# Loading TensorE's address registers for all tiles of a phase at once, in place of one in front of each tile

## The reference, cut to what matters

```
x = _layer_norm(src + attn, ln1_g, ln1_b)
keys = (x @ router_w + router_b)[..., 0]
expert_idx = jnp.remainder(jnp.floor(keys).astype(jnp.int32), N_EXPERTS)
for e in range(N_EXPERTS):
    h = jax.nn.relu(x @ W1[e] + b1[e])          # 128 -> 512
    y = h @ W2[e] + b2[e]                       # 512 -> 128
    ff_out = ff_out + jnp.where((expert_idx == e)[..., None], y, 0.0)
return _layer_norm(x + ff_out, ln2_g, ln2_b)
```

## Time and profile before

| | |
|---|---|
| median of 3 runs | 363.2 us (363.07 to 365.33) |
| profiled execution | 363.53 us |
| its span | 361.7 us, so 1.8 us lie around it |
| TensorE busy | 277.0 us (77%) |
| VectorE busy | 243.1 us (67%) |
| ScalarE busy | 176.1 us (49%) |
| GpSimd busy | 144.8 us (40%) |
| 16 DMA engines | 65 GB/s on average |

### The profile page before, as it was taken

How to read it: one execution, slowest core, us unless ns; L and a number is a source line. 1 busy time by engine, 2 the same in 40 slices (tenths; PEclk the granted TensorE clock), 3 DMA queues, 4 the chain that set the end, 5 groups by cost and what they waited for, 6 DMA issues and landing times.

```text
span 361.7 us, 9124 instructions
## 1 busy us (share of the span) xinstructions
PE 277.0 (77%) x3299; PEld 209.8 (58%) x3299; DVE 243.1 (67%) x677; ACT 176.1 (49%) x352; POOL 144.8 (40%) x333
## 2 busy tenths in 40 slices
PE   2665686786876826898689999998986997869970
PEld 1243454455554513576377757677865777768860
DVE  5997698888798594365257648768751465737781
ACT  2323988977998763244534624463331132314420
POOL 2126566556466360131024005703300421655665
PEclk9998889988998987699899989999997598869995
DMA  5899900000000000000000000100300352465410
GB/s 151 233 338 336 287 3 1 0 2 0 0 3 2 0 0 2 0 4 2 2 2 3 5 2 2 63 2 32 92 18 2 98 164 63 120 181 164 142 53 19
DMA packets 21875, 23.42 MB, mean 65 GB/s; under 512 B 1826, under 2 KB 18496, under 8 KB 21832
## 3 DMA queue, kind: packets, MB, share of 16 engines
q1 hardware_dynamic: 17720, 14.68, 13.8%
q10 hardware_dynamic: 2736, 4.98, 4.8%
q0 software_dynamic: 1376, 3.18, 2.5%
HBM read 10.74 MB, written 12.29 MB: 64 GB/s over the span
## 4 chain that ended last, share of the span: by engine, by line
PE 44%; DVE 27%; POOL 12%; issue 9%; ACT 3%; DMA 2%; DVEq 1%; POOLq 1%; ACTq 0%; SPq 0%
PE bank L802 9%; PE scores L775 7%; PE scores L772 6%; DVE mneg L1371 5%; POOL ln_tmp L456 5%; DVE pair_st L1251 5%; DVE early L1245 4%; PE scores L931 4%; PE bank L946 4%; PE bank L614 3%; PE bank L708 2%; DVE early L1263 1%; PE scores L640 1%; DVE early L346 1%; DVE st L278 1%
## 5 line engine op out<-in xcount | busy, mean ns | idle before, releaser
L1099 ACT ACTIVATE probs<-scores 128x1024 f32<-128x1024 f32 x32 | 32.8, 1025 | 67.0 <-PE scores L779 67.0
L1371 DVE TENSOR_REDUCE mneg<-scores 128x8 bf16<-128x1024 f32 x32 | 39.2, 1224 | 26.9 <-PE scores L772 23.6
L1245 DVE TENSOR_TENSOR_SCAN early<-a_both,bank 128x512 f32<-128x512 f32 x32 | 38.9, 1215 | 4.6 <-issue 4.3
L1379 DVE RECIPROCAL sums<-bank 128x128 f32<-128x128 f32 x16 | 15.3, 958 | 32.9 <-PE bank L802 32.8
L431 POOL TENSOR_SCALAR a_both<-early 128x508 f32<-128x508 f32 x32 | 19.5, 611 | 34.9 <-ACT early L1005 31.0
L779 PE MATMUL scores<-mnegT,pick 32*128 32x128 bf16 x256 | 30.4, 224 | 0.0
L653 PE MATMUL scores<-ident,early 128*128 128x128 f32 x64 | 16.8, 329 | 15.7 <-DVE early L1263 14.8
L1156 ACT ACTIVATE h_bwd<-bank,vec 128x128 f32<-128x128 f32 x19 | 8.7, 457 | 40.6 <-PE bank L614 36.5
L614 PE MATMUL bank<-ident,early 128*128 128x128 f32 x136 | 24.2, 308 | 3.9 <-DVE early L346 1.6
L456 POOL TENSOR_TENSOR ln_tmp<-ln_tmp,minus_half 128x8 f32<-128x8 f32 x16 | 26.4, 1648 | 1.3
L653 PEld LDWEIGHTS scores<-ident,early 128*128 128x128 f32 x64 | 10.4, 170 | 27.1 <-issue 27.1
(11 more groups left out here) (239 smaller groups left out, 766.9 us busy)
## 6 DMA issues: line engine op xcount, KB each, us to landing
sorted_rows<-blank SPq DMA_DIRECT2D x1, 8710.0 KB, 31.7
w_of<-in_L_ffn_W_dram ACTq DMA_DIRECT2D x19, 256.0 KB, 2.8
late<-sorted_rows SPq DMA_DIRECT2D x15, 130.0 KB, 2.8
x_rows<-in_x_dram SPq DMA_DIRECT2D x4, 256.0 KB, 3.1
w_s<-in_L_ffn_W_dram SPq DMA_DIRECT2D x4, 256.0 KB, 3.7
x_rows<-sorted_rows SPq DMA_DIRECT2D x4, 130.0 KB, 2.4
ctx_rows<-in_ctx_dram SPq DMA_DIRECT2D x1, 256.0 KB, 3.2
ctx_rows<-in_L_ffn_b_dram SPq DMA_DIRECT2D x1, 256.0 KB, 31.7
```

The costliest lines, as they stand in the source:

```text
L1099: act.activation(probs[:, n % 2, :, :].rearrange("p (i h j) q -> p h i j q", i=2, j=4)[:, 1 - h], exp_banks, ACT.Exp, scale=SCALE).then_in ...
L1245: dve.tensor_tensor_scan(out_s, a, b, 0.0, ALU.mult, ALU.add).then_inc(s["s_ready"], 1)
L1371: dve.tensor_reduce(mneg[:, n % 2, h::2, 0:4], max_banks, AX.X, ALU.max, negate=True).then_inc(s["mx_r"], 1)
```

## The change

`choose(i)` goes, and `choose_phase(b)` comes in its place. It waits once for the entries of phase b and loads the registers of all its tiles one behind another: five, four and ten. It stands where the load of the phase's first tile stood, between `turn_tile` and `hidden`. The registers of a phase live until the `output` of their tiles. Nothing else differs: the other engines' instructions are the same, and TensorE has as many as before.

```
-            def choose(i):
-                if i in first_slot[:-1]:
-                    pe.wait_ge(s["steer_r"], phase_of(i) + 1)
-                chosen[i] = pe.value_load(steer[0:1, 0, i:i + 1], min_val=0, max_val=(NE - 1) * DFF)
+            def choose_phase(b):
+                pe.wait_ge(s["steer_r"], b + 1)
+                for i in range(first_slot[b], first_slot[b + 1]):
+                    chosen[i] = pe.value_load(steer[0:1, 0, i:i + 1], min_val=0, max_val=(NE - 1) * DFF)
 
             turn_tile(0)
             weighted_values(NT - 1)
             for i in range(-1, NS):
                 if i + 2 < NS:
                     turn_tile(i + 2)
+                if i + 1 in first_slot[:-1]:
+                    choose_phase(phase_of(i + 1))
                 if i + 1 < NS:
-                    choose(i + 1)
                     hidden(i + 1)
```

## The result

The changed kernel takes 372.4 us (median of 4 runs, 372.14 to 376.26) against 363.8 us before (4 runs, 363.07 to 365.33). The ratio is 1.0256, with a 95% interval of 1.018 to 1.0332: slower by 8.6 us at the medians. The profiled execution took 372.19 us, its span is 370.4 us against 361.7, so the two spans differ by 8.7 us and the two traces show the whole of it. Some executions of a kernel take longer at a lower clock; the ratios and intervals here leave these out, the medians don't, so that the two can differ a little.

What follows compares the result with a forecast made beforehand. The expert stage was taken as bound by the path from L614 over ScalarE's copy and ReLU to L946, not by the loads; 363.5 + 7.5 (0 + 2.2 + 0 + 4.2 + 1.1) = 371.0 us, range 367.5 to 373.5.

Steps and rivals of the forecast that it cites:

- The loads removed bring 0 us: Tiles of a phase: removing loads before L931 saves 0 us, since L946 then waits for ScalarE; the period stays 2.40 us.
- 0.65 us for a load in a row: TensorE's sequencer at a phase's start: each load in a row takes 0.65 us, bounded by 0.47 and 0.8 us.
- First phase, +2.2 us: Five loads in place of one: L931 2.4 us late, the shift goes through to tile 9; +2.2 us, 1.0 to 3.3.
- Second phase, 0 us: Four loads in place of one before L931 of tile 5: 1.95 us, hidden by TensorE's wait for tile 9's DMA.
- Third phase, +4.2 us: Ten loads in place of one hold L931 of tile 9 until 329.3, today 325.09: +4.2 us, 2.4 to 5.7.
- The clock after it, +1.1 us: Behind the third row TensorE resumes at half clock for some 5 us: +1.1 us, 0.3 to 1.8.
- The sum: Whole kernel: 0 + 2.2 + 0 + 4.2 + 1.1 = 7.5 us more, 371.0 us.
- That the products pass the loads: Rival: the queue takes L931 while the sequencer still loads, so only 0.6 us is won; about 363.0 us, chance 0.08.
- That the idle time was the bound: Rival: rows run hidden under queued matmuls and all 4.8 us of idle time come back; 358.7 us, chance 0.04.
- That the rows cost but the period shrinks: Rival: the rows cost, but ScalarE starts L1156 earlier and 2.6 us come back; 368.4 us, chance 0.12.
- That only the third phase pays: Rival: the first phase's shift vanishes in TensorE's own waits of the routing chain; 368.8 us, chance 0.14.

## Why the prediction was right, and where it wasn't

**The loads removed bring 0 us:** right. From the turn of tile 11 to that of tile 18, 7 tiles, it is 16.86 us before (327.93 to 344.79) and 16.93 after (336.62 to 353.55), and with the load behind L931 the period is 2.41 us as well. One reading behind it was incomplete: it counted the load's 0.36 us as TensorE's own. The kernel with the ReLU first shows that this depends on how far the sequencer is ahead of the engine: with 0.8 us the load takes nothing, with 0.4 us L931 waits 0.26 us.

**0.65 us for a load in a row:** right for the third phase (5.9 us for nine steps), too low for the first, where the four steps from 288.7 to 291.7 take 3.0 us in place of 2.6.

**First phase, +2.2 us:** the term that was mis-sized. It measured 3.6 us at the turn of the last group's rows and 3.7 at the turn of tile 9, above its upper end of 3.3. The same stretch of the kernel before, weight loads from 289 us on, wasn't among the rows:

```profile
289.67 1.03 PEld L931 LDWEIGHTS scores<-h_bwd,w_of 128*128 128x128 f32 x8
291.22 0.97 PEld L811 LDWEIGHTS bank<-wo_s,att 128*128 128x128 f32 x8 [0.53 <-DVE att L1380]
292.10 0.14 PEld L614 LDWEIGHTS bank<-ident,late 128*128 128x128 f32 x1
```

L931 comes 2.8 us later (292.47), where I had 2.4; 0.2 of it is that the row began at 288.7 in place of 288.5, which is not its own doing. From there to the next turn it is 3.35 us (to 295.82) in place of 2.43: the lower clock costs 1.45, and 0.53 comes back, as L811 had waited that long for VectorE. Another 0.1 comes back at the next tiles: 2.8 + 1.45 - 0.53 - 0.1 = 3.6. The prediction had all of these, the 0.5 inside its 1.9 us for L811. It put the clock at up to 1.1 without a working, and so came to 2.8 at most, and then took 2.2, as if half the clock's price were enough. It came whole, and at 1.45.

Behind that turn the shift did not go through unchanged, as the prediction had it. It shrinks to 2.9 us at the scatter and 2.6 at the issue of tile 9, and grows to 3.7 with the 1.1 us that tile 9's DMA took longer, for which the sum had no term. That the 2.2 lies near the 2.6 is luck: 1.4 us too little up to the turn, and 1.0 that came back behind it. The kernel with the first row alone, 3.4 us by its time (1.5 to 5.2), can't tell 2.2 from 3.6.

**Second phase, 0 us:** right, by the kernel with that row alone as far as its time can tell, and by its trace. In the full change TensorE still waits 1.33 us for tile 9. Had that tile landed after 2.5 us, as before, some 0.2 us of the wait would be left (an estimate): the cover was just long enough.

**Third phase, +4.2 us:** right, 4.2 us, and by its steps: the row starts 2.1 us behind the turn of tile 9 (322.6 for 320.47 before, 326.3 for 324.19 after), ten loads take 6.5, the waits behind them 0.2. What I had not foreseen is that TensorE's own work there would run at the full clock (from the turn of tile 9 to that of tile 10 it takes 2.36 us, 324.19 to 326.55). It changes the idle time, 6.34 us where I had some 4, and not the delay, as the kernel with the third row alone shows, with the lower clock, 4.16 us of idle time and the same delay. With the ReLU first the sequencer reaches the row 1.2 us behind that turn (the turn at 322.73, the loads from 323.9), and L931 comes 7.9 us behind it in place of 8.85.

**The clock after it, +1.1 us:** 0.75 us (7.95 to 8.7 late).

**The sum,** 7.5 us, against 8.7 in the profiled executions and 8.6 at the medians; of the miss of 1.2 us, 1.5 belong to the first phase, with 1.1 of them come by the DMA of tile 9, and -0.3 to the clock behind the third.

**The rivals.** That the products pass the loads: out, L931 waits 6.34 us in front of queued work that needs no register. The Trainium skill's page "Advanced Engine Details and Errata", section Sequencer and Instruction Queues, says that other engine instructions can be read and queued while a control instruction executes. The trace disagrees for products that stand behind such loads in the same stream: L931 started 0.3 us after the last of the ten was through, having waited 6.34 us. That the idle time was the bound: out, by the period. That the rows cost but the period shrinks: out, 2.41 us as before; the period fell only where ScalarE's order was changed. That only the third phase pays: out, by the first row alone.

## What to carry over

An idle time in front of an instruction is worth removing only if the next one isn't held by something else; read the whole period, from one turn to the next, and look for a tile in which the idle time is already absent. Small sequencer work spread between products hid here beside another engine's path; collected in a row it cost 0.65 us a load wherever nothing else covered it, and the products behind it ran at the lower clock. If such work shows up as idle time, look for the wait that keeps the sequencer from running ahead: here two calls of another engine, swapped, brought 1%, and the load moved behind one product perhaps another 0.5% (ratios of 0.985 twice against 0.990, with intervals that overlap).

## What the runs showed that I had not expected

The first three loads of the row beside the end of the attention took 493, 491 and 374 ns, later ones 293 to 309 but for one of 388. Most of the excess of the first row's steps is this, and what makes them slow was not tried.

The clock's low stretches don't stand where they stood. The end of the attention ran at 1.00 after the change, with TensorE busy 1.70 of 3.50 us, where before it had run at 0.50, busy all of 3.50 us (286.0 to 289.5 in both), and the two products after the idle time at 0.50. The begin of the stage moves between executions of kernels that are alike up to there: the turn of tile 1 came between 288.6 and 294.4 us in the profiled executions. The landing of single DMAs moves too: the last part of the scatter took 2.4 to 5.8 us, tile 9 2.0 to 3.6. A difference of 1% in one profiled execution need therefore not be the kernel's, and only the distances from one milestone to the next, beside repeated times, carried the argument here.
